# Decoder layer, feed-forward stage: token maxima over stored rows, cross-attention products ahead of the shuffle wait, rounding in one VectorE step

## The reference, cut to what matters

```python
x = _layernorm(x + attention(x, ...))            # x1
query = einsum('bnc,dc->bnd', ctx, Wq) + bq
key = einsum('bnc,dc->bnd', ctx, Wk) + bk
attention = softmax(einsum('bnd,bmd->bnm', query, key))
x = _layernorm(x + einsum('bln,bmn->blm', x, attention))     # x2
def act_quant(x):
    scale = 127.0 / clip(max(abs(x), axis=-1, keepdims=True), EPS)
    return clip(round(x * scale), -128.0, 127.0) / scale
def h_bitlinear(x, w):                           # w ternary
    return act_quant(fwht(x)) @ weight_quant(w).T
gate = h_bitlinear(x, w_gate)                    # 512 -> 2048
up = h_bitlinear(x, w_up)
x = _layernorm(x + h_bitlinear(silu(gate) * up, w_down))     # 2048 -> 512
```

## Time and profile before

| | us |
|---|---|
| median of 3 runs | 1225.28 (1222.91 to 1225.84) |
| the profiled execution | 1230.77 |
| span of its profile | 1229.0 |
| TensorE matmuls busy | 969.5 |
| VectorE busy | 860.4 |
| ScalarE busy | 694.1 |
| GpSimd busy | 373.8 |

### The profile page before, as it was taken

How to read it: one execution, slowest core, us unless ns; L and a number is a source line. 1 busy time by engine, 2 the same in 40 slices (tenths; PEclk the granted TensorE clock), 3 DMA queues, 4 the chain that set the end, 5 groups by cost and what they waited for, 6 DMA issues and landing times. The chain is left out here.

```text
span 1229.0 us, 13431 instructions
## 1 busy us (share of the span) xinstructions
PE 969.5 (79%) x4128; PEld 366.9 (30%) x4128; DVE 860.4 (70%) x1624; ACT 694.1 (56%) x1106; POOL 373.8 (30%) x296
## 2 busy tenths in 40 slices
PE   1556478988999888988988578988897799779565
PEld 0222112222222222222222243334443444334222
DVE  6854468888888998999896548837764776475245
ACT  2775425777777767776767224436633663365255
POOL 1000135546566567565301243122003101310000
PEclk9878668999999998999999879989998999899877
DMA  9873154555555555555523321321052105102500
GB/s 333 279 281 132 46 165 138 156 168 179 169 179 174 173 156 173 162 173 157 156 64 109 117 77 26 68 44 69 3 129 42 69 18 125 29 1 51 119 1 35
DMA packets 90798, 145.80 MB, mean 119 GB/s; under 512 B 12356, under 2 KB 52164, under 8 KB 89095
## 3 DMA queue, kind: packets, MB, share of 16 engines
q1 hardware_dynamic: 87270, 132.36, 36.6%
q10 hardware_dynamic: 3456, 12.58, 2.9%
HBM read 85.54 MB, written 42.21 MB: 104 GB/s over the span
## 5 line engine op out<-in xcount | busy, mean ns | idle before, releaser
L1134 DVE TENSOR_REDUCE neg_max<-banks 128x1 f32<-128x512 f32 x512 | 332.1, 683 | 55.1 <-PE banks L978 52.4
L1083 ACT ACTIVATE probs<-banks 128x512 f32<-128x512 f32 x512 | 278.9, 598 | 120.4 <-PE banks L996 115.8
L996 PE MATMUL banks<-q_st,k_st 99*128 99x512 bf16 x512 | 196.8, 387 | 34.1 <-ACT probs L1083 27.7
L978 PE MATMUL banks<-k_st,q_st 96*128 96x512 bf16 x512 | 201.6, 398 | 4.3 <-DMA k_st<-qk_parts 2.3
L1010 PE MATMUL banks<-probs,v_st 128*32 128x512 f32 x1024 | 138.2, 612 | 8.9 <-ACT pv_z L1107 7.7
L1670 PE MATMUL banks<-q_T,f_int_all 128*128 128x512 bf16 x512 | 125.8, 387 | 19.5 <-DVE h_ring L1691 19.4
L1464 POOL TENSOR_TENSOR rstd<-vare,half 128x1 f32<-128x1 f32 x48 | 26.8, 558 | 358.2 <-DVE vare L1456 358.2
L1729 PE MATMUL banks<-hz,I_h 128*128 128x512 f32 x128 | 71.3, 698 | 35.3 <-DMA hz<-h_turned 32.9
L996 PEld LDWEIGHTS banks<-q_st,k_st 99*128 99x128 bf16 x512 | 49.8, 98 | 133.5 <-ACT probs L1083 72.5
L978 PEld LDWEIGHTS banks<-k_st,q_st 96*128 96x128 bf16 x512 | 50.9, 100 | 127.5 <-DVE neg_max L1134 64.8
L1301 POOL TENSOR_SCALAR woT<-woT 128x1024 f32<-128x1024 f32 x24 | 87.2, 3632 | 2.4 <-ACT woT L1295 0.4
(11 more groups left out here) (260 smaller groups left out, 1506.7 us busy)
## 6 DMA issues: line engine op xcount, KB each, us to landing
hz<-h_turned SPq DMA_DIRECT2D x64, 256.0 KB
f_int_all<-in_ffn_dram ACTq DMA_DIRECT2D x24, 512.0 KB, 6.9
woT<-in_ffn_dram SPq DMA_DIRECT2D x24, 512.0 KB, 3.7
qk_parts<-parts SPq DMA_DIRECT2D x32, 384.0 KB, 2.5
q_st<-qk_parts SPq DMA_DIRECT2D x32, 384.0 KB, 3.9
k_st<-qk_parts SPq DMA_DIRECT2D x32, 384.0 KB, 4.9
qk_parts<-parts SPq DMA_DIRECT2D x32, 256.0 KB, 2.8
pv_rows<-pv_z SPq DMA_DIRECT2D x32, 256.0 KB, 5.1
```

What stands on the lines that cost most here:

```text
L978: pe.matmul(s_bank[tile % SB], q_st[g.i][0:KR, j, qt * P:(qt + 1) * P], k_st[g.i][0:KR, j, :], start=True, stop=True).then_inc(s_mm, 1)
L996: pe.matmul(st_bank[i], k_st[g.i][:, j, kt * P:(kt + 1) * P], q_st[g.i][:, j, :], start=True, stop=True).then_inc(st_mm, 1)
L1083: act.activation(probs[ktp][:, j, i, :], st_bank[i], ACT.Exp).then_inc(exp_done, 2)
L1134: dve.tensor_reduce(neg_max[:, g.h, tile:tile + 1], s_bank[tile % SB], AX.X, ALU.max, negate=True).then_inc(max_done, 1)
```

## The change

- The absolute values go. act_h2 only copies the pair back to hz. dve_max now reads four stored rows of hz at once, in one tensor_reduce with absolute value, 512 groups of four elements 2 KB apart; for the second to fourth set of rows a fold into h_max follows. The waits on h_abs become waits on h2_sb.
- xm 0 and xm 1 move into iterations 14 and 15 of the first half, xm 2 and xm 3 to behind the last H128 product, with the first turn and the first Hadamard step of batch B behind them, all ahead of the wait for the shuffle. O_AT and TURN_AT come one iteration earlier.
- Token tiles 1 and 3 of hz are scaled on GpSimd, from a copy of the multiplier rows that ScalarE makes in SBUF. VectorE scales tiles 0 and 2.
- Rounding becomes one VectorE instruction per tile, with both additions, that writes the bf16 result. ScalarE's two passes go.
- pe_top comes behind pe_row1.

```diff
         def pe_xm(pe, B, n, bank):
-            need(pe, "x1_T_sb", 4 * B + n + 1)
+            need(pe, "x1_T_sb", 4 * B + (n + 1 if B == 0 else KD))
...
             def act_h2(act, b, p):
                 need(act, "h2_mm", 8 * b + p + 1)
                 did(act.copy(hz[:, 2 * p:2 * p + 2, :], pair_banks(p)), "h2_sb")
-                need(act, "maxed", 16 * b + 2 * p)
-                need(act, "bias_o_ready", 2)
-                did(act.activation(h_abs[:], pair_banks(p), ACT.Abs), "h_abs")
...
+            def dve_max(dve, b, q):
+                rows = hz[:, 4 * q:4 * q + 4, :].rearrange("p a t -> p t a")
+                need(dve, "h2_sb", 8 * b + 2 * q + 2)
+                need(dve, "top_mm", b)
+                if q == 0:
+                    did(dve.tensor_reduce(h_max[:], rows, AX.X, ALU.max, apply_absolute_value=True), "maxed")
+                else:
+                    need(dve, "maxed", 4 * b + q)
+                    link(dve, dve.tensor_reduce(h_part, rows, AX.X, ALU.max, apply_absolute_value=True))
+                    did(dve.tensor_tensor(h_max[:], h_part, h_max[:], ALU.max), "maxed")
...
+            def act_mul(act, b):
+                need(act, "row2_mm", b + 1)
+                need(act, "scaled2", 2 * b)
+                need(act, "scaled2_pool", 2 * b)
+                did(act.copy(mul_row, MUL_BANK), "mul_sb")
...
+            def pool_scale2(pool, b, t):
+                tile = hz[:, :, token_tile(t)]
+                need(pool, "mul_sb", b + 1)
+                did(pool.tensor_tensor(tile, tile, mul_row[:, token_tile(t)].unsqueeze(1).to_broadcast([P, FK, P]),
+                                       ALU.mult), "scaled2_pool")
...
+            def dve_q2(dve, b, t):
+                i = 4 * b + t
+                need(dve, ("scaled2", "scaled2_pool")[t % 2], 2 * b + t // 2 + 1)
+                need(dve, "d_mm", i - 3)
+                did(dve.tensor_scalar(q2_T[:, :, token_tile(t)], hz[:, :, token_tile(t)], MAGIC, -MAGIC, ALU.add,
+                                      ALU.add), "q2_ready")
...
-            O_AT = {3: 0, 6: 1, 9: 2, 12: 3}
-            TURN_AT = {5: 0, 8: 1, 11: 2, 14: 3}
+            O_AT = {2: 0, 5: 1, 8: 2, 11: 3}
+            TURN_AT = {4: 0, 7: 1, 10: 2, 13: 3}
+            XM_AT = {14: 0, 15: 1}
...
                         pe_x1_T(pe, B, TURN_AT[i], FRONT)
+                    if B < NB and i in XM_AT:
+                        pe_xm(pe, B, XM_AT[i], FRONT)
...
-                    if b and i < 4:
-                        dve_scale2(dve, b - 1, i)
+                    if b and i in (1, 2):
+                        dve_scale2(dve, b - 1, 2 * i - 2)
+                    if b and 2 <= i < 6:
+                        dve_q2(dve, b - 1, i - 2)
...
+                    if B < NB and i == FK - 1:
+                        dve_xm(dve, B, 0, FRONT)
...
+                    if b and i in (1, 2):
+                        pool_scale2(pool, b - 1, 2 * i - 1)
...
             def pe_second(pe, b):
                 B = b + 1
...
+                for i in range(FK - LAG1, FK):
+                    pe_h1(pe, b, i)
+                pe_xm(pe, B, 2, FRONT)
+                pe_xm(pe, B, 3, FRONT)
+                pe_t2(pe, B, 0)
+                pe_had(pe, B, 0)
                 pe_h2(pe, b, 0)
                 pe_h2(pe, b, 1)
...
             def dve_second(dve, b):
                 B = b + 1
...
+                dve_quant1(dve, B, 0)
                 dve_max(dve, b, 0)
+                dve_quant1(dve, B, 1)
                 dve_max(dve, b, 1)
+                dve_quant1(dve, B, 2)
                 dve_max(dve, b, 2)
...
                 dve_quant1(dve, B, 3)
                 dve_tok1(dve, B)
+                dve_max(dve, b, 3)
                 dve_quant2(dve, b)
```

More of the change, by code:

```diff
@@ L1698, in pe_h1 @@
                 elif i == 1:
[L1699 removed]
+                    need(pe, "scaled2", 2 * b)
                 if i >= 2:
@@ L1996, in act_second @@
             def act_second(act, b):
                 B = b + 1
-                for i in range(12, 16):
+                for i in range(FK - LAG1, FK):
                     act_y(act, b, i)
+                act_t2(act, B, 0)
                 act_h2(act, b, 0)
                 act_h2(act, b, 1)
-                act_t2(act, B, 0)
+                act_t2(act, B, 1)
                 act_h2(act, b, 2)
+                act_w1(act, B, 0)
+                act_t2(act, B, 2)
                 act_h2(act, b, 3)
-                act_t2(act, B, 1)
@@ L2102, in _ @@
                         act_h2(act, b, p)
-                    for t in range(KD):
-                        act_round2(act, b, t)
-                        act_q2(act, b, t)
+                    act_mul(act, b)
                 @block.gpsimd
@@ L2148, in _ @@
                     dve_first(dve, b)
-                    for p in range(8):
-                        dve_max(dve, b, p)
+                    for q in range(4):
+                        dve_max(dve, b, q)
                     dve_quant2(dve, b)
                     dve_scale2(dve, b, 0)
-                    dve_scale2(dve, b, 1)
+                    dve_q2(dve, b, 0)
+                    dve_scale2(dve, b, 2)
+                    dve_q2(dve, b, 1)
+                    dve_q2(dve, b, 2)
+                    dve_q2(dve, b, 3)
                     for t in range(KD):
-                        if t + 2 < KD:
-                            dve_scale2(dve, b, t + 2)
                         dve_final(dve, b, t)
```

100 lines of the change are left out of this document (28 added, 72 removed).

## The result

The changed kernel takes 1259.12 us (median of 4 executions, 1254.22 to 1263.41) beside 1225.56 us of the kernel before (now four executions too): a ratio of 1.0274, 95% interval 1.0224 to 1.0324. It is slower, and outside the range of the forecast. The profiled execution is the fastest of the four, 1254.22 us with a span of 1252.4, so 23.4 us above that of before.

What follows compares the result with a forecast made beforehand. Bound by a chain of waits: TensorE after a VectorE-set start, the rate-limited shuffle, then a mixed stretch. Batches -1.0, +0.4, +0.4, -6.7, clock +5.7 and loads +1.0 gave -0.2 us: 1225.1, range 1209 to 1239.

Steps and rivals of the forecast that it cites:

- The unknown price: VectorE's strided reduction of 2048 elements in the maxima: range 2.3 to 4.9 us, taken 3.75.
- The wait before xm 1: TensorE idle 3.0 us before the second cross-attention product, until VectorE has read the first from the shared bank.
- T to S: Last down product's end to first H16 product after the shuffle: +9.3 us batch 0, +8.7 batches 1 and 2, -3.9 batch 3.
- the maxima: Batch 3, after its first H16 product: faster products without absolute values, against four reductions and three folds, -0.1 us.
- the end: Last batch, scaling, rounding and four down products after the multiplier rows: 21.9 us against 25.2, -3.3 us.
- VectorE from S: the first stored rows are there at 4.6: VectorE's first maximum can start 4.6 us after the first H16 product that follows the shuffle.
- S to G: First H16 product after the shuffle to the next batch's first gate product: 28.0 us against 38.4, -10.3, batches 0 to 2.
- That puts the up product at G+16.6 ... T is G+62.2: First gate product to fifth up product 16.6 us, to last down product's end 62.2: +2.0 batches 1 and 2; batch 3 +0.6.
- the clock at xm 1 and at S: TensorE's clock falling after idle before xm 1 and the first H16 product: 0.8 and 1.1 us, 5.7 over three batches.
- clock and loads: +5.7 us for TensorE's low clock after idle times, +1.0 for later x and attention loads in batches 0 and 1.
- rival 3: Slower by the moved products: clock falls in full at both idle times, 13 us more, 1238; chance 0.15.
- the forecast's two cases: VectorE's rounding beside GpSimd's product waits 0.8 us if next, 3.8 more if GpSimd's next instruction goes first.

Runs made afterwards that it cites:

- Run 9: Run 7's kernel with GpSimd's inverse deviations ahead of the second butterfly and H16 pairs 5 and 7 copied before the waiting w1 rounding: ratio 0.9943 to before.
- run 1: Changed kernel with GpSimd computing the inverse deviations of token tiles 2 and 3 ahead of the previous tile's second butterfly: 1255.71 us.
- run 3: Changed kernel with scaling of all four token tiles back on VectorE, each followed by its rounding, in iterations 1 to 4: 1259.95 us.
- run 11: Changed kernel with reductions reading four neighbouring elements instead of four 2 KB apart, so the maxima are not the right ones: 1236.94 us.
- run 10: Changed kernel with scaling on VectorE, rounding in two ScalarE passes for batches 0 to 2 and on VectorE in the last: ratio 1.0178 to before.
- run 6: Kernel before with only xm 2, the first turn and first Hadamard step moved ahead of the shuffle wait, later small steps reordered: 1223.3 us.
- run 7: Changed kernel with xm 0 and xm 1 put back behind H128 products 13 and 15: 1235.51 us.

## Why the prediction was wrong

**Right.** The unknown price, taken at 3.75 us, was 3.68 to 3.75. The wait before xm 1 is there, 3.02 us for 3.0, released by its read. T to S in batch 2 is 29.8 for 29.6. Batch 3: T to S -4.1 (-3.9), the maxima -1.2 (-0.1), the end -2.9 (-3.3).

**Wrong,** in the order of size, against the profiled execution, which is 23.4 us slower where the sum said -0.2:

1. *"VectorE from S: the first stored rows are there at 4.6"*, and with it S to G -10.3. Measured: -5.2, -3.7 and -5.1, so 16.9 us are missing in three batches, 1.4 of them the low clock at S in batch 1. The rows were there (ScalarE's first two copies end at S+4.7), VectorE was not: it came 3.3 us late from GpSimd's queue and lost 1.75 us more at ScalarE's. Run 9 shows it: with the orders mended, S to G is 27.2. The forecast took the moved turn past the queues of TensorE, ScalarE and VectorE and not past that of GpSimd, whose second butterfly waits for it. The timeline of GpSimd in the kernel before has that wait, at its old length:

```profile
1063.23 1.41 POOL L1557 TENSOR_TENSOR y<-y4a 128x256 f32<-128x256 f32 x2 [1.75 <-PE banks L1576]
```

2. *"That puts the up product at G+16.6 ... T is G+62.2"*, +2.0. Measured +5.8 and +5.6, and +4.4 for +0.6 in batch 3: 11.2 us missing. The up product came at G+17.9, since GpSimd's products took 4.5 us each where 3.8 was taken: 1.3 us. The larger part, 2.4 us a batch, is a term that was not in the sum. Its G+16.6 already held TensorE waiting there, but not the clock behind the wait: behind 7.07 us of idle time it was at 0.50, with 1.89 us for an up product of 1.04 and 3.3 us to the end of the down products behind it in place of 1.7. In batch 3, behind 4.52 us, the split is 1.6 and 2.2.
3. *T to S, +9.3, +8.7 and +8.7.* Measured +10.6, +11.8 and +8.9, 4.7 us more, nearly all of it from the low clock at xm 1, which took 5.3, 6.6 and 3.7 us. The sum had 5.7 us for the clock at xm 1 and at S on a line of its own, and in this profile the two cost 4.5 and 1.4: right, but by luck. In runs 1, 3 and 11 xm 1 ran at 0.50 in both later batches, or nearly (5.4 to 6.7 us). In run 10 it was high in all three batches behind the same idle times. Two executions of the changed kernel were 8 to 9 us slower than the profiled one, with a mean granted clock of 0.903 and 0.904 where it had 0.911; that they lost it at the same places is likely, and no profile shows it.

Together 16.9 + 11.2 + 4.7, less the 6.7 allowed for clock and loads, less 2.1 for an earlier first G and 0.4 for batch 3's other parts and the time behind its last product: 23.6 us on top of the forecast -0.2, so the 23.4 measured.

The forecast bought S to G with T to S, and rival 3 ("slower by the moved products") priced their clock alone. The trade itself was the mistake of the change: xm 0 and xm 1, put back, give 4.6 us in batch 2 (29.8 to 25.2), where xm 1 had the high clock, and 7.4 in batch 1, where it had not. What gained is xm 2, the first turn and the first Hadamard step behind the last H128 product (run 6); xm 3 beside them was too much for the wait and put 4.3 us into T to S (run 7).

VectorE's rounding waited for whole instructions of GpSimd. In batch 2 the rounding asked at 999.70, GpSimd's second product ended at about 1001.7 (992.70 + 9.03), the rounding at 1002.8, 1.1 us later. In the last batch it asked at 1226.90, in GpSimd's first product, and ended at 1230.16; GpSimd's two products took 9.98 us there and not 9.03. So it came between them: it did not wait for the second. This agrees with the rule that the forecast took from the Trainium skill, SBUF — State Buffer, in its part on the engine ports, and of the forecast's two cases it is the one in which the rounding comes next.

## What to carry to other kernels

When a step of one engine is moved past a long wait, follow every queue that waits for that step, also the engines that look idle: here a GpSimd butterfly, two ScalarE copies and the place of the last H16 pair cost 5.5 us a batch (run 9 against run 7), where the move was to gain 10.3. Work that fills a wait belongs behind the last thing that feeds that wait, not ahead of it, and no more of it than the wait holds; the placing was worth 24 us here (run 7). And each new idle time of TensorE, wherever it arises, gets a price for the clock behind it: 2.4 us a batch here at a place that the sum had not looked at.

## What the runs showed of the hardware

- The rounding, which reads and writes SBUF, was held up by GpSimd, and the scaling, which reads its multipliers from PSUM, was not: the rounding took 1.23 us alone and 3.11 and 3.26 us beside a GpSimd product, the scaling 2.28 us beside one and alone. GpSimd waits as well: its two products took 9.03 us, and 9.98 where a rounding came between them.
- The same 3.02 us of idle time ahead of the same product left TensorE's clock high in batch 2 and at 0.50 for 6 us in batch 1. Behind 7.07 us it was low in both batches; behind 4.16 us, in batch 0, low in the kernel after (up product 1.89 us) and high in run 10 (1.04 us); behind 2.55 us before the last down tile, high in the kernel before (3.63 us) and low in run 6 (5.29 us). So the length of the idle time alone did not decide it.
- A reduction of 2048 f32 elements in groups of four takes 2.29 us if the four are neighbours and 3.68 if they lie 2 KB apart (run 11 and the kernel after). The Trainium skill, Advanced Engine Details and Errata, Memory Cachelines, speaks of a penalty where each access is in another line; these rows agree, and its size is from them.
